# A fused four-layer transformer kernel: the first attention's query projection in units of one head by four token tiles, three steps ahead, and the middle stage's variance from ScalarE sums

## The reference

```
x = x + xattn0(ln(x), ctx)   # 32 heads of 128, 4 KV groups, keys = context + own tokens, softmax
x = x + ffn0(ln(x))          # dense 512x512 + top-2 of 28 LoRA experts of rank 8
x = x + xattn1(ln(x), ctx)   # 32 heads, 8 KV heads, RMS-normed q and k, softmax
x = x + ffn1(ln(x))          # dense + top-2 of 8 experts of rank 8
x = x + xattn2(ln(x), ctx)   # linear attention: softmax(q), exp(k), k^T v, 8 features a head
x = x + ffn2(ln(x))          # top-2 of 4 experts of rank 16
x = x + xattn3(ln(x), ctx)   # one head of 512
x = x + ffn3(ln(x))          # clustered dense layer
```

## Time and profile before

| | |
|---|---|
| median of 3 runs | 1515.21 us (1513.29 to 1516.6) |
| profiled execution, its own time | 1514.17 us |
| its span | 1512.4 us |
| mean granted TensorE clock | 0.996 |
| PE, DVE, ACT, POOL busy | 1468.0, 1046.0, 916.6, 395.5 us |
| query units in psQ, 768 matmuls of 256 columns | 99.6 us busy |
| query units in psTP, 768 matmuls of 256 columns | 97.5 us busy |

### The profile page before, as it was taken

The page is one execution under the profiler, slowest core; times in us unless marked ns, Lnnn a source line. Parts: engine busy times, 40 slices in busy tenths (PEclk is TensorE's granted clock), DMA queues, the critical chain, the costliest instruction groups (busy, mean ns, idle before and its releaser), DMA issues.

```text
span 1512.4 us, 27886 instructions
## 1 busy us (share of the span) xinstructions
PE 1468.0 (97%) x9532; PEld 1311.2 (87%) x9532; DVE 1046.0 (69%) x2472; ACT 916.6 (61%) x3101; POOL 395.5 (26%) x454
## 2 busy tenths in 40 slices
PE   8999999999999999998999999999999999988997
PEld 7999999999999998886888888888888888877885
DVE  6566655655665567886777777777777788779776
ACT  4455445545564555546777777777777775455652
POOL 5102010201020102233232323232323242554431
PEclk9999999999999999999999999999999999999999
DMA  6100100010000100101110111101010101011101
GB/s 217 36 29 29 43 29 29 29 42 29 29 29 29 42 29 28 56 36 43 36 43 36 43 40 39 50 29 50 29 50 29 40 8 68 22 53 36 50 15 59
DMA packets 16114, 62.59 MB, mean 41 GB/s; under 512 B 2228, under 2 KB 3764, under 8 KB 10984
## 3 DMA queue, kind: packets, MB, share of 16 engines
q1 hardware_dynamic: 15976, 60.82, 11.6%
HBM read 58.72 MB, written 2.10 MB: 40 GB/s over the span
## 4 chain that ended last, share of the span: by engine, by line
PE 38%; DVE 8%; ACT 4%; issue 2%; POOL 1%; ACTq 0%; POOLq 0%; DVEq 0%
PE psQ L870 9%; PE psY L954 9%; PE psKV L894 5%; PE psSO L941 2%; PE psSO L839 2%; PE psTP L904 2%; ACT prob L1481 1%; PE psSO L840 1%; PE psKV L1287 1%; PE psQ L1241 1%; ACT pT L1396 1%; PE psTP L924 1%; PE psQ L795 1%; DVE bn L1924 1%; PE psSO L1270 1%
## 5 line engine op out<-in xcount | busy, mean ns | idle before, releaser
L954 PE MATMUL psY<-wo,oT 128*128 128x512 f32 x1536 | 378.1, 394 | 0.7 <-DVE oT L1902 0.2
L954 PEld LDWEIGHTS psY<-wo,oT 128*128 128x128 f32 x1536 | 278.8, 188 | 56.1 <-POOL wo L541 2.2
L1396 ACT ACTIVATE pT<-psTP 64x256 fp32r<-64x256 f32 (+1 forms) x192 | 86.8, 452 | 142.8 <-PE psTP L924 142.1
L541 POOL TENSOR_TENSOR wo<-stage_o,wo 128x512 fp32r<-128x512 f32 x68 | 87.2, 1311 | 310.3 <-ACT wo L1396 279.6
L1484 ACT ACTIVATE prob<-wide,neg_mx 128x128 f32<-128x128 f32 x256 | 99.7, 391 | 79.0 <-DVE neg_mx L2034 79.0
L1481 ACT ACTIVATE prob<-s_sb,neg_mx 128x64 f32<-128x64 f32 x256 | 85.9, 337 | 94.5 <-DVE neg_mx L2034 94.5
L1902 DVE TENSOR_TENSOR pT<-psTP,pT 64x256 fp32r<-64x256 f32 (+1 forms) x192 | 97.6, 508 | 64.5 <-ACT pT L1396 62.7
L661 POOL TENSOR_TENSOR rms<-ms_eps,minus_half 128x5 f32<-128x5 f32 (+1 forms) x64 | 74.2, 1159 | 230.8 <-DVE ms_eps L2047 230.0
L894 PEld LDWEIGHTS psKV<-wkv,arena 128*128 128x128 f32 x768 | 100.3, 190 | 7.0 <-DVE kT L2082 1.9
L894 PE MATMUL psKV<-wkv,arena 128*128 128x256 f32 x768 | 102.6, 283 | 1.2 <-DVE kT L2082 1.2
L870 PE MATMUL psQ<-wq,hT 128*128 128x512 f32 x384 | 103.7, 407 | 0.0
(11 more groups left out here) (322 smaller groups left out, 3481.5 us busy)
## 6 DMA issues: line engine op xcount, KB each, us to landing
stage_o<-in_wo SPq DMA_DIRECT2D x16, 1024.0 KB, 4.8
stage_q<-in_wq SPq DMA_DIRECT2D x15, 1024.0 KB, 5.1
stage_kv<-in_wkv SPq DMA_DIRECT2D x12, 512.0 KB, 3.5
stage_q<-in_ctx SPq DMA_DIRECT2D x16, 256.0 KB, 2.9
stage_o<-in_ctxT SPq DMA_DIRECT2D x2, 1024.0 KB, 4.8
stage_q<-in_base SPq DMA_DIRECT2D x2, 1024.0 KB, 5.0
stage_kv<-in_ctx SPq DMA_DIRECT2D x8, 256.0 KB, 3.1
out<-x_res SPq DMA_DIRECT2D x8, 256.0 KB, 2.2
```

Source lines behind the costliest of these rows:

```text
L541: g.tensor_tensor(dst[LO], stage, dst[HI].bitcast(f32), ALU.subtract).then_inc(ld[done or what + "_lo"], 1)
L954: m = mm(psY[:], oT[:, ol, h, :], wo[:, wl, h, :], start=h == 0 and i == 0, stop=h == HQ - 1 and i == 2)
L1396: copy = lambda o, i: nc.scalar.activation(o, i, ACT.Copy)
```

## The change

1. Query units. The first 8 units stay as they are. From unit 8 on a unit is *one head and four tiles*: 12 matmuls of 512 columns. Its place moves from one step ahead to three: TensorE makes unit t+3 in step t (`units_of`; a second unit in steps 4 and 6), so steps 61 and 62 have none. ScalarE and VectorE write the two parts of two units in each even step and none in an odd one (`units_kept`): the first where it stood, the second after `exps` and after `normalise`.
2. Storage. Queries of all heads of a group and four tiles lie in one buffer (`pairs`, 16 KB a partition), which reuses the place of xn, kT1, v1 and qT; tiles 6 and 7 of the first norm and 0 to 4 of the second use q_sb for xn.
3. New wq weights are written in steps 5, 12, 20, ..., 52. Two slices stand at the start of ScalarE's step, ahead of `pT_hi`, the other two later; GpSimd now writes three low slices and VectorE one. New wkv weights: steps 14, 30, 46 in place of 12, 28, 44.
4. Middle. `ln_stats(5)`, the statistics within `gates` and the two `stats_after` leave VectorE. The residual sum becomes one `scalar_tensor_tensor` that also gives the row sum; ScalarE makes sum((sum - 512 x)^2) by a Square activation (`deviations`, 16 of them), and GpSimd scales it.

```diff
+    def by_pairs(k):
+        return k.t < NT
...
+    def units_of(t):
+        early = {0: (0, 1), 1: (2,), 2: (3,), 3: (4,), 4: (5, 6), 5: (7,), 6: (8, 9), 7: (10,), 8: (11,)}
+        return [unit(k) for k in early.get(t.t, (t.t + 3,)) if k < STEPS]
+    def units_kept(t):
+        early = {0: (0, 1), 1: (), 2: (2, 3), 3: (4,), 4: (5, 6), 5: (7,)}
+        return [unit(k) for k in early.get(t.t, () if t.t % 2 else (t.t + 2, t.t + 3)) if k < STEPS]
+    def units_before(n):
+        return n // 2 * 2 + 2 if n < NT else n // 4 * 4 + 4
+    def changes_wq(t):
+        return t.exists and t.t in (5, 12, 20, 28, 36, 44, 52)
...
-                pe.wait_ge(s["qT_lo"], u.c + (1 if a.rms else 2 - u.res(2)))
+                pe.wait_ge(s["qT_lo"], u.c + 1 if a.rms else units_before(u.t))
...
+                    parts = [(unit_bank(k)[:].rearrange("p (n t) -> p n t", n=4), k.t % 4)]
+                for out, h in parts:
+                    head = slice(h * HD, (h + 1) * HD)
...
+                new_wq = not a.rms and changes_wq(t)
+                if new_wq:
+                    next_wq(t, 0, 1)
                 if t2.exists:
                     pT_hi(t2)
...
-                for k in units[-1:]:
+                for k in units[:1]:
                     unit_hi(k)
...
                 if t1.exists:
                     exps(t1)
+                for k in units[1:]:
+                    unit_hi(k)
...
+        def deviations(ln, n):
+            ...
+            nc.scalar.activation(unused, x[:, n], ACT.Square, bias=mv[:, n, 0:1], scale=-float(D),
+                                 accum_out=mv[:, n, 1:2]).then_inc(LNS[ln]["var"], 1)
...
             if 1 <= t <= 4:
                 kvs_hi(t - 1)
+            if 0 <= e - 2 < NT:
+                deviations(6, e - 2)
+            if 0 <= t - 3 < NT:
+                deviations(5, t - 3)
             if 0 <= t - 1 < NT:
                 act.wait_ge(s["nmr"], t)
...
                 if t1.exists:
                     normalise(t1)
+                for k in units[1:]:
+                    unit_lo(k)
...
+            return V.scalar_tensor_tensor(x[:, n], bank[:], 1.0, x[:, n], ALU.mult, ALU.add, accum_out=mv[:, n, 0:1])
...
-            if 0 <= t - 3 < NT:
-                dve.wait_ge(s["x_add"], t - 2)
-                ln_stats(5, t - 3)
...
-                gates(f, e, e - 2 if e > 1 else None, 6)
+                gates(f, e)
```

More of the change, by code:

```diff
@@ L120, in build @@
     oT = sb("oT", [2, HQ, P], f32r)
-    xn = sb("xn", [2, D])
     ident = sb("ident", [P])
@@ L304, in norms_of, with alone, xn_of @@
         return [0, 1] if t == 4 else [t - 3]
-    def xn_slot(ln, n):
-        return {5: 1, 6: 0, 7: 0}.get(ln, n % 2)
+    def alone(ln, n):
+        return ln == 0 and n > 5 or ln == 1 and n < 5
+    def xn_of(ln, n):
+        return q_sb[:] if alone(ln, n) else xn[:, {5: 1, 6: 0, 7: 0}.get(ln, n % 2)]
     def ln_bank(ln, n):
@@ L587, in low_wq, with low_wq0 @@
                 low("wq", halves(wq, k), stage[:, k], load * 4 + (k + 1))
+        def low_wq0(load):
+            low_wq(load)
+            low("wq", halves(wq, 2), stage_q[:, 2], load * 4 + 3, "wq_lo_v")
         def low_wo(count, n=KT):
@@ L603, in _ @@
         ln_rstd(0, 1)
-        low_wq(0)
-        low("wq", halves(wq, 2), stage_q[:, 2], 3, "wq_lo_v")
+        low_wq0(0)
         ln_rstd(0, 2)
@@ L998, in attention @@
                         kv_proj(t)
-                    if t1.exists and units:
+                    if t1.exists and not ending:
                         scores(t1)
@@ L1555, in attention @@
                 next_wo = a.rms and t.res(8) == 2 and t.t < STEPS
-                units = [] if a.rms else units_of(t)
-                scores_first = not a.rms and not units
+                units = [] if a.rms else units_kept(t)
+                scores_first = not a.rms and t.t >= STEPS - 1
                 if scores_first:
@@ L1570, in attention @@
                     squares(t)
-                for k in units[:-1]:
-                    unit_hi(k)
+                if t.t == 0 and units:
+                    unit_hi(units.pop(0))
                 if a.index == 0 and t.static and t.t == 0:
@@ L2161, in attention @@
                     gates(FF[1], 0)
-                for k in units[:-1]:
-                    unit_lo(k)
+                if t.t == 0 and units:
+                    unit_lo(units.pop(0))
                 between = first if t.static and t.t == 0 else ()
```

156 lines of the change are left out of this document (102 added, 54 removed).

## The result

The changed kernel takes 1517.84 us (median of 20 runs, 1515.53 to 1519.97), the kernel before 1515.41 (median of 20). The ratio is 1.0018, with a 95% interval of 1.0011 to 1.0024: 2.4 us slower, less than the 0.2% named as the bound of "the same". The forecast was +2.7 us, 1517.9. The profiled execution of the changed kernel took 1518.43 us, with a span of 1516.7, so it stands 4.3 us of span over the profiled one of before. The runs say which part of that is the change.

The account below looks back on a forecast made before the run. PE bounds the first attention, chains through DVE and ACT the middle. Terms -7.3 + 5.5 + 0.2 - 1.3 + 4.3 + 1.3 = +2.7 us, so 1517.9 us on the median; range 1511.5 to 1523.5.

Parts of the forecast that it names:

- Width: First attention: 56 units of 512-column matmuls take 2.75 us each in place of 2.88, -7.3 us.
- Two units ahead: First attention: two more units precede the scores of step 58; steps 61 and 62 give nothing back, +5.5 us.
- Late end: End of the first attention: one late copy for unit 63, less a removed PE wait for queries, about +0.2 us.
- wq: First attention: writing new wq weights earlier removes PE's waits for them, -1.3 us.
- Second copy: Even steps: the second copy delays oT or kT behind wo, seven steps at 0.6 us, +4.3 us.
- wq's new place: Two slices ahead of pT_hi delay it about 1 us, covered by score and output products: no cost.
- Middle, DVE and ACT: Middle: ScalarE's sums delay gate_exp, DVE's relief mostly buys nothing, +1.3 us; bounds -6.5 and +4.
- The term of -0.7 at p = 0: Middle, p = 0: two stats_after leave the path from last expert sum to k_product, about -0.7 us.
- The adds: Middle: the three-operand residual sum takes 0.75 us against 0.68, +0.07 for each of 8 critical adds.
- PE's idle time in step 62: Sign in the first attention: PE idle over 3 us in step 62 behind DVE's prob.
- C: Rival, middle: DVE's relief reaches the end, -6.5 us in place of +1.3, 1510.1 us; chance 0.14.
- B: Rival, end of first attention: clock falls in steps 61 and 62, about +2.6 us more, 1520.5; chance 0.20.

Follow-up runs that it names:

- middle_only: The kernel before with only the middle stage changed, first attention as before: 1516.93 us, ratio 1.0009 to the kernel before.
- attn_only: The changed kernel with the middle stage of the kernel before: 1517.08 us, ratio 1.0012 to the kernel before.
- fill: The changed kernel plus 12 matmuls of 512 columns, results unread, in each of steps 61 and 62: 1519.3 us, ratio 1.0020 to the kernel before.
- best_old: The changed kernel with fewer second copies, earlier start copies, last four units as before, three copies ahead of row_max, and the old middle: 1511.95 us.
- small_sums: The changed kernel with each of ScalarE's 16 sums over one column in place of 512: 1518.04 us, ratio 1.0018 to the kernel before.
- late_sums: The changed kernel with ScalarE's middle-step sums moved from ahead of q_exp to behind gate_exp: 1521.04 us, ratio 1.0035 to the kernel before.

## Why the prediction was right, and where it was not

The total, +2.7 against +2.4, is right, and so is the share of the attention: +1.4 forecast (all terms but the middle's), +1.5 in the runs and +1.65 by starts. The middle, +1.3 forecast, has +1.3 in the runs of middle_only, +0.8 between attn_only and the changed kernel, and about nothing by the starts; so its size is not shown. The terms hold less well than their sum.

- *Width, -7.3:* -7.0 in the runs, -6.3 by starts up to step 60. Right, from the row of like shape and neighbour. The -1.7 that follows from the formula of the Trainium skill (TensorE: Matmul & The Clock Gate, Back-to-back issue gap), which gives it for a single matmul by itself, does not agree with it.
- *Two units ahead, +5.5:* right. Steps 4 and 6 are 2.89 and 2.57 us longer, 5.46. Nothing comes back in steps 61 and 62: 5.5 us of work put there cost nothing (fill).
- *Late end, +0.2:* +0.35 by starts.
- *wq, -1.3:* mis-sized. I took the three idle times of the earlier trace rows as the price. But steps 15, 31 and 47, from one output projection to the next, lasted 8.83 us before and 7.57 now, 1.26 less, of which 0.13 are the width: 3 x 1.1 = -3.4. The unit of step 15 in the kernel before shows it:

```profile
153.51 0.52 PE L855 MATMUL psQ<-hT,wq 128*128 128x256 f32 x3
154.46 3.22 PE L855 MATMUL psQ<-hT,wq 128*128 128x256 f32 x21 [0.44 <-POOL wq L541]
157.52 0.60 PE L924 MATMUL psTP<-ident,prob 128*128 128x128 f32 x4
```

  From 153.51 to 157.52 are 4.01 us in place of 2.88: 1.13, of which the row names 0.44. The 21 matmuls behind the wait take 3.06 us where 21 x 0.12 = 2.5 are due; PE went on with gaps that no row names.
- *Second copy, +4.3:* mis-sized. Seven steps at 0.48, +3.4, net 2.7. The places were right, the waits for oT 0.33 us each and not 0.5. The same in kv steps, which I took as an estimate, is 0.47.
- *wq's new place, at nothing:* this step failed. I said that two slices ahead of pT_hi delay the pT copy, and that the output projection covers it. It does. But queued behind them is also the unit's copy, through row_max: in step 12 it ends at 145.6, and the unit of step 13 needs its bank. The step is 8.24 us long in place of 7.57: +2.0 in three steps (13, 29, 45), and some 0.15 each in steps 21, 37 and 53. Of the lateness 0.65 us is another collision with GpSimd, which here writes its three low slices of wq. The last instruction of row_max takes 0.82 us in place of 0.17 and ends with the third slice; DVE, then POOL:

```profile
144.19 0.82 DVE L2124 TENSOR_SCALAR neg_mx<-mx 128x4 f32<-128x4 f32 x1
144.92 0.68 DVE L1992 TENSOR_TENSOR heads_of_four<-psQ,heads_of_four 128x512 fp32r<-128x512 f32 x1
```

```profile
141.18 3.80 POOL L583 TENSOR_TENSOR wq<-stage_q,wq 128x512 fp32r<-128x512 f32 x3 [5.27 <-ACT wq L1447]
```

  Without it the copy would have ended at 144.95, ahead of 145.26, when PE began to wait; that was not tried by itself, since best_old moves the copy ahead of row_max (its step 13 takes 7.90 us). The kernel before has the same 0.83 us in step 14, where no bank waits for it.
- *Start, not in the sum:* `units_kept` leaves out step 1, so unit 4 waits for unit 2's bank: +0.8, and 1.5 more where the clock falls.
- *Middle, DVE and ACT, +1.3:* the sign and the place (L2063 3.74 us behind kvs, 3.5 by the sum) were right, with 1.6 us over three steps. The term of -0.7 at p = 0 is there too: from the last MAX8 of the gates to the end of the span are 117.8 us in the changed kernel and 118.4 before. The adds were priced at 0.07 each and cost nothing: DVE's READ_ACCUMULATOR stands in the trace with 0.08 us, and the next instruction starts 0.60 us behind the add, as before. And two collisions with GpSimd, 0.93 us each, were in no term; the step with the first is 0.1 us longer than before. By starts the middle comes out even; the runs of middle_only have it at +1.3, half of it with the clock.

So +2.0 and +0.8 that I had not seen were met by 2.1 us more from wq and 1.6 less from the second copy. With the sizes measured the attention's terms add up to 1.4 us (2.1 with the width by starts), against 1.65. The total was right partly by luck. Of the signs that I named, PE's idle time in step 62 was 2.7 us and not over 3. Of the rivals, C (DVE's relief reaches the end) falls with small_sums, in which ACT is nearly out of the way: at the gates of step 11, ahead of the collisions, it stands 0.4 us ahead of the kernel before, counted from the last projection, where C's gains up to there are 5.5. B was right in that the clock falls in steps 61 and 62, and wrong in its price.

## What to carry over

When a copy or a load is moved on an engine, follow each thing that is queued behind it to its *last* reader, the next writer of the same bank among them: here it was not the probabilities but a PSUM bank that was late. Take the price of a wait from the length of the step with it and without it, not from the idle time that the view gives to it. And where a value comes sooner, others start sooner on it: look up what they meet then, before busy time taken from an engine is booked as a gain.

## What the runs showed of the hardware

- A DVE instruction of 128 x 4 elements with two inputs in SBUF took 1.13 to 1.22 us in place of 0.20 to 0.22 while GpSimd split slices of 128 x 512 from SBUF (2.54 us for two), and ended with a slice: at 1393.89 beside 1393.84 in the changed kernel. Where the slices came behind it (late_sums) it took 0.22. Those behind it, with one input in PSUM, took their usual 0.28 and 0.68 us beside the second slice. A `tensor_scalar` of 128 x 4 with one input in SBUF was held as well, 0.82 in place of 0.17. The Trainium skill (SBUF — State Buffer, SBUF: two separate sides) has DVE and GpSimd share a pair of ports under an exclusive lock, held for the whole instruction. The numbers agree: the delay is 0.93 us, less than one slice of 1.27.
- A DVE sum output costs no time: READ_ACCUMULATOR 0.08 us, hidden. On ACT the next instruction starts 0.70 to 0.72 us behind a sum of 128 x 512, as it does behind an activation of this size without one (0.71, `ln_norm_act` at 1345.40), though ACTIVATION_READ_ACCUMULATOR stands in the trace with 0.19. The 0.92 us of steps 7 and 8 is the kernel's wait.
- The clock of one kernel differs between executions, and stretches of 3.4 us at 1.2 GHz appear in places with the same code. One cost 1.5 us in step 3, some 1.1 in the middle, at most 0.3 where DVE led, and nothing at 700 us. Where it followed PE's idle stretches of steps 61 and 62, it came in eight of eight profiles.
